# Three-stage audio tower on one core: the first stage hands beta to GpSimd and a filter tap to ScalarE, and VectorE's order in the third stage changes

## The reference

```python
# layer 1: pad to 768, keep every second row: 3 segments of 128 tokens, 256 wide
probs = softmax(x @ x.T / 16);  h = probs @ x
# layer 2, on layernorm(h), 384 tokens, 4 heads of 64
q, k, v = (silu(causal_dwconv4(xn @ W)) for W in (Wq, Wk, Wv))
beta = sigmoid(xn @ Wb)
delta = delta_rule(l2norm(q), l2norm(k), v * beta, k * beta)      # chunks of 32, triangular inverse
fir_short = causal_dwconv(v, 3 taps); fir_long = causal_dwconv(v, 63 taps)
w = softmax over 4 branches of mlp([xn, mean and deviation of each branch])
h = h + rmsnorm(w0*fir_short + w1*fir_long + w2*delta + w3*v) * o_norm_w @ Wo
# layer 3, on layernorm(h): 6 experts, the best 2 by a router; all six are computed
h = h + sum_e weight_e * (gelu(y @ w1_e) @ w2_e)
```

## Time and profile before

| | us |
|---|---|
| median of 3 runs (2374.53 to 2377.92) | 2375.09 |
| the profiled execution, its own time | 2393.8 |
| its span in the profile | 2392.1 |
| PE busy | 2251.9 (94%) |
| DVE busy | 1852.8 (77%) |
| ACT busy | 1290.8 (54%) |
| POOL busy | 555.5 (23%) |

### The profile page before, as it was taken

The page is one execution under the profiler, slowest core; times in us unless marked ns, Lnnn a source line. Parts: engine busy times, 40 slices in busy tenths (PEclk is TensorE's granted clock), DMA queues, the critical chain, the costliest instruction groups (busy, mean ns, idle before and its releaser), DMA issues.

```text
span 2392.1 us, 53303 instructions
## 1 busy us (share of the span) xinstructions
PE 2251.9 (94%) x20796; PEld 1635.1 (68%) x20796; DVE 1852.8 (77%) x5111; ACT 1290.8 (54%) x2632; POOL 555.5 (23%) x413
## 2 busy tenths in 40 slices
PE   5999999999799779999999999999999999999997
PEld 4666666666587666777677767776776677767765
DVE  4999999999868367677778777777777667767765
ACT  4888888888624334544454455445544544454452
POOL 1444444444400011121112111111111121112111
PEclk9999999999958879999999999999999999999999
DMA  3776777777778912233224222322233224222300
GB/s 98 231 245 229 229 241 245 236 238 236 247 241 314 378 60 71 71 108 96 78 70 139 91 77 71 125 81 74 70 132 105 71 70 133 77 71 76 125 21 21
DMA packets 224297, 334.44 MB, mean 140 GB/s; under 512 B 113870, under 2 KB 190766, under 8 KB 215342
## 3 DMA queue, kind: packets, MB, share of 16 engines
q1 hardware_dynamic: 219726, 309.01, 39.1%
q10 hardware_dynamic: 2304, 12.58, 1.3%
q0 software_dynamic: 2016, 9.44, 1.0%
HBM read 191.66 MB, written 164.23 MB: 149 GB/s over the span
## 4 chain that ended last, share of the span: by engine, by line
PE 49%; DVE 7%; ACT 6%; issue 4%; POOL 0%; DVEq 0%
PE bank L1662 7%; PE bank L1672 7%; PE bank L1595 6%; PE bank L1475 4%; PE bank L1555 4%; PE bank L1632 4%; PE bank L1571 2%; PE bank L1507 2%; PE bank L1543 2%; ACT L1808 2%; ACT L1803 2%; DVE v_all L2111 1%; PE bank L1503 1%; PE bank L1485 1%; DVE DL L2019 1%
## 5 line engine op out<-in xcount | busy, mean ns | idle before, releaser
L2111 DVE SCALAR_TENSOR_TENSOR v_all<-bank,we,v_all 128x256 f32<-128x256 f32 x576 | 264.9, 476 | 219.3 <-PE bank L1672 214.3
L739 DVE SCALAR_TENSOR_TENSOR Y<-bank,convw,Y 128x383 f32<-128x383 f32 (+2 forms) x576 | 330.6, 602 | 3.2 <-ACT Y L627 2.9
L1672 PE MATMUL bank<-w2e,HE 128*128 128x256 f32 x1152 | 327.9, 395 | 2.4 <-DVE v_all L2111 2.3
L1662 PE MATMUL bank<-v_all,w1e 128*128 128x384 f32 x768 | 289.6, 500 | 2.4 <-ACT HE L1808 2.3
L445 PE MATMUL bank<-pb,wqkv 128*128 128x384 f32 x768 | 282.4, 491 | 1.8 <-DVE Y L739 1.8
L1672 PEld LDWEIGHTS bank<-w2e,HE 128*128 128x128 f32 x1152 | 198.0, 191 | 55.3 <-issue 19.3
L1808 ACT ACTIVATE HE<-bank 128x384 f32<-128x384 f32 x192 | 94.1, 490 | 248.9 <-PE bank L1662 248.2
L1595 PE MATMUL bank<-v_all,w1g 128*128 128x384 f32 x512 | 193.4, 500 | 2.0
L1662 PEld LDWEIGHTS bank<-v_all,w1e 128*128 128x128 f32 x768 | 134.5, 191 | 75.9 <-issue 19.8
L445 PEld LDWEIGHTS bank<-pb,wqkv 128*128 128x128 f32 x768 | 132.1, 191 | 61.1 <-DVE Y L739 8.3
L1786 ACT ACTIVATE first_stage<-bank 32x384 f32<-32x384 f32 (+1 forms) x192 | 92.2, 480 | 135.7 <-PE bank L1583 119.2
(11 more groups left out here) (217 smaller groups left out, 5199.1 us busy)
## 6 DMA issues: line engine op xcount, KB each, us to landing
packa<-pa SPq DMA_DIRECT2D x32, 1932.0 KB, 6.2
v_all<-packa SPq DMA_DIRECT2D x32, 1932.0 KB, 8.1
packb<-pb SPq DMA_DIRECT2D x32, 768.0 KB, 6.1
v_all<-packb SPq DMA_DIRECT2D x32, 768.0 KB, 10.8
toeplitz<-taps SPq DMA_DIRECT2D x128, 190.0 KB, 5.3
toep<-toeplitz SPq DMA_DIRECT2D x32, 760.0 KB, 7.6
packb<-fsk SPq DMA_DIRECT2D x32, 384.0 KB, 2.7
first_stage<-fl SPq DMA_DIRECT2D x32, 384.0 KB, 8.7
```

The source lines that it names most:

```text
L739: dve.scalar_tensor_tensor(out=Y[:, j, lag:T], in0=proj_bank[j][:, 0:T - lag], scalar=convw[:, j, CK - 1 - lag:CK - lag], in1=Y[:, j, lag: ...
L1662: mm = pe.matmul(bank[6][:, 0:T], w1e[:, a, k, :], YT[s][:, a, :], start=(a == 0), stop=(a == HALF - 1))
L1672: pe.matmul(expert_bank(b), HE[k % 2][:, b * P:(b + 1) * P], w2e[:, k, :], start=True, stop=True)\
L2111: dve.scalar_tensor_tensor(out=HA[s][:, b, :], in0=expert_bank(b), scalar=we[s][:, b, k:k + 1], in1=HA[s][:, b, :], op0=ALU.mult, op1=ALU. ...
```

## The change

In the first stage: `fir_first` moves from VectorE to ScalarE, each half directly behind its head copy or its silu; `finish_beta` moves from VectorE to GpSimd, as a sum with a column of ones and a power of -1, placed between `k_norms` and `keep_v(c, 0)`; TensorE's stream loses waits that other waits already cover, and `transpose_x` moves behind the first half of `project(b, 0)`. In the third stage VectorE's `delta_out(n, 0)` moves ahead of `routing_weights`, `remainder(n, 1)` ahead of `weigh(it, 2)`, and `remainder(n, 2)` ahead of `add_expert(e, 1, 0)` and `add_expert(e, 1, 1)`. All operands, results and sizes stay.

```diff
                 def transpose_x(n):
                     pe.wait_ge(*x_loaded[n % 2].now(n // 2))
-                    pe.wait_ge(*xnT0_copied.before(n))
-                    pe.wait_ge(*xnT1_copied.before(n))
...
                 def scores(n):
                     pe.wait_ge(*xT01_copied.now(n))
-                    pe.wait_ge(*xT2_copied.now(n))
-                    pe.wait_ge(*h_ready.before(n))
                     if n > 1:
                         pe.wait_ge(*hvk_ready.now(n - 2))
+                    else:
+                        pe.wait_ge(*xT2_copied.now(n))
...
-                    if j == 0:
+                    if j == 0 and 0 in halves:
                         pe.wait_ge(*xnT0_copied.now(n))
                         pe.wait_ge(*xnT1_copied.now(n))
-                    pe.wait_ge(*(taps_done(n - 1, j + 3) if j < 3 else taps_done(n, j - 3)))
+                    elif 0 in halves:
+                        pe.wait_ge(*(taps_done(n - 1, j + 3) if j < 3 else taps_done(n, j - 3)))
...
-                    pe.wait_ge(*sq_ready.now(n))
-                    pe.wait_ge(*h_ready.now(min(n + 1, NB - 1)))
-                    pe.wait_ge(*hvk_ready.before(n))
+                    if 0 in part:
+                        pe.wait_ge(*sq_ready.now(n))
...
+                    if 0 <= b < NB:
+                        project(b, 0, (0,))
                     if 0 <= a < NB:
                         transpose_x(a)
-                    if 0 <= b < NB:
-                        project(b, 0, (0,))
...
+                def fir_first(n, a):
+                    act.wait_ge(*silu_done.now(n, 5 + a))
+                    act.wait_ge(*fs_ready.before(n))
+                    act.activation(fsT[:, a, :], VT[:, a, :], ACT.Copy, scale=firw[:, a, FS - 1:FS]).then_inc(fir_begun.sem, 1)
...
                         silu(c, 4)
                         copy_head_values(c)
+                        fir_first(c, 0)
                     if 0 <= a < NB:
                         copy_xT(a)
                     if 0 <= c < NB:
                         silu(c, 5)
+                        fir_first(c, 1)
                         copy_k_tokens(c)
...
-                        fir_first(c, 0)
                         head_sums(c)
-                        fir_first(c, 1)
                         fir_tap(c, 0, 1)
...
-                    if 0 <= c < NB:
-                        finish_beta(c)
...
+                def finish_beta(n):
+                    pool.wait_ge(*eb_ready.now(n))
+                    pool.wait_ge(*vbs_ready.before(n))
+                    pool.tensor_tensor(b1[:, :], eb[:, :], upper[:, P - 1:P].broadcast_to([P, NM]), ALU.add).then_inc(b1_ready.sem, 1)
+                    pool.wait_ge(*b1_ready.now(n))
+                    pool.tensor_tensor(beta[:, :], b1[:, :], minus_one[:, :], ALU.pow).then_inc(beta_ready.sem, 1)
...
                         k_norms(c)
+                        finish_beta(c)
                         keep_v(c, 0)
...
                         gate_weights(it)
+                    if 0 <= n < NB:
+                        delta_out(n, n % 2, 0)
                     if 0 <= e < NB:
                         routing_weights(e, e % 2)
+                    if 0 <= n < NB:
+                        remainder(n, 1)
                     if 0 <= it < NB:
                         weigh(it, it % 2, 2)
-                    if 0 <= n < NB:
-                        delta_out(n, n % 2, 0)
-                        remainder(n, 1)
...
+                    if 0 <= n < NB:
+                        remainder(n, 2)
                     if 0 <= e < NB:
                         add_expert(e, 1, 0)
                         add_expert(e, 1, 1)
                     if 0 <= n < NB:
-                        remainder(n, 2)
                         delta_out(n, n % 2, 1)
```

More of the change, by code:

```diff
@@ L194, in first_phase @@
         mv = sb("mv", [P, BLK, 2])
-        eb, b1, kbs = (sb(f"t{n}", [P, NM]) for n in range(3))
+        eb, b1, kbs, minus_one = (sb(f"t{n}", [P, NM]) for n in range(4))
         beta = sb("beta", [P, NM])
@@ L243, in first_phase @@
         xnT1_copied = signal("xnT1_copied")
-        eb_ready = signal("eb_ready")
-        beta_step = signal("beta_step", 2)
+        eb_ready, b1_ready = signal("eb_ready"), signal("b1_ready")
+        beta_ready = signal("beta_ready")
+        fir_begun = signal("fir_begun", 2)
         tap_done = signal("tap_done", 6)
@@ L256, in first_phase @@
         vtok_copied = signal("vtok_copied")
-        fir_step = signal("fir_step", 6)
+        fir_step = signal("fir_step", 4)
         fs_copied = signal("fs_copied")
@@ L287, in _ @@
                                     upper[q * SC:(q + 1) * SC, P + q * SC:P + (q + 1) * SC]).then_inc(started, 1)
-                dve.wait_ge(started, 11 + NQ)
+                dve.memset(minus_one[:, :], -1.0).then_inc(started, 1)
+                dve.wait_ge(started, 12 + NQ)
             @block.gpsimd
@@ L464, in transpose_head_values @@
                 def transpose_head_values(n):
-                    pe.wait_ge(started, 1)
                     pe.wait_ge(*hv_copied.now(n))
@@ L480, in v_to_tokens @@
                 def v_to_tokens(n):
-                    pe.wait_ge(*silu_done.now(n, 6))
                     pe.wait_ge(*ktok_copied.now(n))
@@ L485, in fir_to_tokens @@
                 def fir_to_tokens(n):
-                    pe.wait_ge(*fir_step.now(n))
                     pe.wait_ge(*vtok_copied.now(n))
@@ L500, in k_kb @@
                     kT, kbT = chans(pa[n % 2], KT), chans(pa[n % 2], KBT)
-                    pe.wait_ge(started, 1)
-                    pe.wait_ge(*kbT0_copied.now(n))
-                    pe.wait_ge(*kbT1_copied.now(n))
+                    if b == 0:
+                        pe.wait_ge(*kbT0_copied.now(n))
+                        pe.wait_ge(*kbT1_copied.now(n))
                     for hh in range(NH // 2):
@@ L602, in exp_beta @@
                     act.wait_ge(*hvk_ready.now(n))
-                    act.wait_ge(*beta_step.before(n))
+                    act.wait_ge(*beta_ready.before(n))
                     act.activation(eb[:, :].rearrange("p (b h) -> p b h", b=BLK), hvk[:, :, 2 * NH:],
                                    ACT.Exp, scale=-1.0).then_inc(eb_ready.sem, 1)
+                def fir_first(n, a):
+                    act.wait_ge(*silu_done.now(n, 5 + a))
+                    act.wait_ge(*fs_ready.before(n))
+                    act.activation(fsT[:, a, :], VT[:, a, :], ACT.Copy, scale=firw[:, a, FS - 1:FS]).then_inc(fir_begun.sem, 1)
                 def copy_k_tokens(n):
@@ L750, in head_sums @@
                                       ALU.add).then_inc(rs_ready.sem, 1)
[L752 to L756, removed]
                 def scales(n):
@@ L760, in scales @@
                     dve.wait_ge(*rr_ready.now(n, 1))
-                    dve.wait_ge(*beta_step.now(n, 2))
+                    dve.wait_ge(*beta_ready.now(n))
                     dve.tensor_tensor(vbs, beta[:, :], RK[:, :], ALU.mult).then_inc(vbs_ready.sem, 1)
@@ L764, in scales @@
                     dve.tensor_tensor(kbs[:, :], vbs, RK[:, :], ALU.mult).then_inc(scales_ready.sem, 1)
[L766 to L769, removed]
                 def fir_tap(n, a, lag):
-                    dve.wait_ge(*fir_step.now(n, 2 * (lag - 1) + a + 1))
+                    dve.wait_ge(*(fir_begun.now(n, a + 1) if lag == 1 else fir_step.now(n, a + 1)))
                     dve.scalar_tensor_tensor(out=fsT[:, a, lag:T], in0=VT[:, a, 0:T - lag],
```

## The result

The changed kernel takes 2392.36 us (median of 6 runs, 2383.86 to 2403.39) against 2376.13 us for the kernel before, both medians of six: ratio 1.0066, 95% interval 1.0045 to 1.0086, so 16 us by the medians. A second measurement of the same two kernels, 12 runs against 23, gave 2389.64 against 2378.99, ratio 1.0033 (1.0007 to 1.0059). The forecast was 2385.7 us, slower by 10.6, in a range from 2364 to 2394.

A forecast was written before the change was run, and what follows sets the result against it. The prediction took a loop through VectorE and ScalarE to bound the first stage, TensorE the third by busy time. +9.6 us (first stage) and +1 us (third) gave +10.6 on the median 2375.09: 2385.7 us, range 2364 to 2394.

The forecast's parts named there:

- What bounds the kernel: First stage: a loop through VectorE and two stretches of ScalarE is as long as a block; VectorE has hardly any gap.
- Beta: First stage: about 0.5 us leaving VectorE turns into waiting for the divides, worth 0; on GpSimd beta is in time, cost 0.
- The tap on ScalarE: First stage: at 0.45 us per tap, last_tap and tap(b, 0, 1) come later; +0.32 us a block, +9.6 us in all.
- The new place of transpose_x: First stage, TensorE: half projection and transposes swap between the same neighbours, off the loop; worth 0, a few hundredths a block.
- the first stage's term: First stage's part of the forecast sum: 30 blocks at +0.32 us, +9.6 us, all from the tap on ScalarE.
- Fewer waits: First stage, TensorE: the waits left out are already met by TensorE's order or a stricter wait; worth 0.
- Third stage: Products held up by GpSimd's delay expert_out by 0.5 us, against 0.3 to 0.5 saved; net +0.03 a block, +1 us.
- The walk: Third stage in time order: first routing product held until 1210.24, remainder ends 1212.1, updates about 1212.15, expert_out 1213.5 instead of 1213.01.
- That the port plays no part: Rival, third stage: the last routing product's 1.07 us has another cause; TensorE gains 1.0 us a block; 2354 us, chance 0.07.
- that the first product slips past GpSimd's: Rival, third stage: first routing product starts before GpSimd's, only the last is held; -0.43 a block, 2371.7 us, chance 0.17.
- That VectorE alone bounds the first stage: Rival, first stage: ScalarE's extra work hides in its idle 1.69 us; -1.15 us a block, 2341 us, chance 0.08.
- that everything lands in slack: Rival, both stages: TensorE's tidier stream and a shorter ScalarE tap win back the 0.32; 2375 +- 4 us, chance 0.16.

The follow-up runs named there:

- the run of beta alone: Kernel before plus beta on GpSimd and fewer TensorE waits; filter tap on VectorE, transposes of x first, third stage as before: 2376.37 us, ratio 0.9995, first-stage block 19.07 us.

## Why the prediction was right, and where not

Point by point, by its own steps.

*What bounds the kernel.* Right. (In the profile's 40 slices VectorE is at nine tenths or more in slices 2 to 10, not 2 to 11; nothing rests on it.) The loop from silu(c, 4) through last_tap, find_max, the exponentials, the divides and row_stats sets the block, and not VectorE's busy time: beta's 0.5 us gained 0.06, and the change as a whole took 1.15 us a block from VectorE and lost 0.36.

*Beta.* Right in kind and size: "worth 0", measured 0.06 a block together with the missing waits; the sum on GpSimd took 0.21 where I had 0.5, and beta was over a microsecond early.

*The tap on ScalarE.* Right mechanism, this term of the sum mis-sized; the slot is 0.51 and 0.52 where I took 0.45 from the bounds 0.40 to 0.60. tap(b, 0, 1) came 0.45 late in the loop and not 0.32; the change's block grew by 0.36, and that of this edit, counted from the run of beta alone, by 0.43.

*The new place of transpose_x.* This is the step that failed: "the half projection and the transposes swap between the same neighbours. Worth 0". TensorE was not on my loop, but VectorE's x copy is, right in front of the filter taps, and the transposes ended only 0.37 us before it began, while the half projection put ahead of them takes 0.75. Alone the swap costs 0.30 to 0.35 a block, about 10 us. That the first stage's term came out near all the same (9.6 forecast, 11.3 measured) is luck: the tap's delay runs beside the swap's and the longer one decides. Fewer waits as such were not run alone; with beta's move they make up the 0.06.

*Third stage.* The mechanism was right: first routing product 1.23, last 1.00, GpSimd's second 1.50, no wait before q_state, a new one before expert_out. The walk also implies the wait of 0.44 before updates, which the prediction does not name. The size was off, by 0.19 a block: -0.16 instead of +0.03. I took weigh's distance as 0.98, from a row where it started together with GpSimd's product; in the changed kernel it is 0.87 (1212.87 to 1213.74), so the expert sum came sooner. With the two blocks laid side by side at GpSimd's first product (1208.71 before, 1209.63 now), expert_out (1214.26) starts at 1213.34 in the walk's times, where the walk has 1213.5. So the third stage won 5 us where I had it lose 1. That and the longer ScalarE slot have opposite signs, and the sum by blocks is +6 where I said +10.6. That the second measurement's 11 us fall on the forecast is luck: by blocks the first stage's term was off by +2 us and the third stage's by -6.

*Rivals.* That the port plays no part and that the first product slips past GpSimd's both fell by the 1.23. That GpSimd's product is the cause of the 1.07 is shown by the run that moves it: 0.17 and 0.18. Why three filter taps with two SBUF inputs run at full pace beside a power was not tried. That VectorE alone bounds the first stage fell by the run of beta alone (19.07, not 18.6), and that everything lands in slack by the longer block.

What stays open: why the second stage of one execution lasts 178 us and of another 207, and whether the changed kernel's first stage shifts those chances. One trace a kernel doesn't decide it.

## What to carry to other kernels

Where a busy engine and a less busy one meet in a loop, walk the loop before moving work: time taken from the busy engine is worth only what no other chain of the loop already takes, and work given to the "idle" engine is free only if its idle time lies behind the new work, not ahead of it. Undo parts one at a time and then in pairs, since two delays side by side hide each other. When two engines hold each other up on large products, put every result that a third engine waits for ahead of the clash: here that won 1.4%, while moving the clash to another product won nothing.

## What the hardware showed that I had not expected

- One VectorE product of 18 elements a partition took 0.17 or 1.23 us by its place alone. What one product saves by not meeting GpSimd's, another pays: with the routing products at 0.17 and 0.18, weigh went from 0.95 to 2.20 us.
- A power of 12 elements a partition on GpSimd took 2.27 us, and a sum of the same size 0.21, eleven times less; I had put the sum at 0.5.
- Half a projection moved ahead of six transposes, with TensorE's total work unchanged, made the kernel 0.56% slower.
